# Attention value products issued in batches of up to eight key blocks, with twelve pairs of probability buffers, one buffer for the values and one for the copied row sums

## The reference, cut to what matters

```python
scores = jnp.einsum('brgtd,bgsd->brgts', qg, k) / jnp.sqrt(jnp.float32(HD))
bias = jnp.tril(diff)[None, None] * slopes[:, :, None, None]
causal = idx[None, :] <= idx[:, None]
scores = jnp.where(causal[None, None, None], scores + bias[None], -jnp.inf)
attn = jax.nn.softmax(scores, axis=-1)
out = jnp.einsum('brgts,bgsd->brgtd', attn, v)
...
gate = jnp.einsum('th,nh->tn', xt, Wg)
up = jnp.einsum('th,nh->tn', xt, Wu)
gelu = jnp.tanh(0.7978845608028654 * (gate + 0.044715 * gate ** 3)) * gate * 0.5 + gate * 0.5
inter = gelu * up
out = jnp.einsum('tn,hn->th', inter, Wd)
...
x = x + _L0_attn_ref(xn, ...) + _L0_ffn_ref(xn, ...)
```

## Time and profile before

| | |
|---|---|
| median of 3 runs | 1785.41 us (1784.62 to 1787.19) |
| the profiled execution's own time | 1784.39 us |
| its span, first to last instruction | 1782.6 us |
| TensorE busy | 1693.1 us (95%), 10368 matmuls |
| VectorE busy | 1340.1 us (75%) |
| ScalarE busy | 1075.6 us (60%) |
| GpSimd busy | 953.2 us (53%) |
| mean granted TensorE clock | 0.985 of full speed |

### The profile page before, as it was taken

How to read it: one execution, slowest core, us unless ns; L and a number is a source line. 1 busy time by engine, 2 the same in 40 slices (tenths; PEclk the granted TensorE clock), 3 DMA queues, 4 the chain that set the end, 5 groups by cost and what they waited for, 6 DMA issues and landing times. The chain is left out here.

```text
span 1782.6 us, 31010 instructions
## 1 busy us (share of the span) xinstructions
PE 1693.1 (95%) x10368; PEld 848.4 (48%) x10368; DVE 1340.1 (75%) x2785; ACT 1075.6 (60%) x1779; POOL 953.2 (53%) x801
## 2 busy tenths in 40 slices
PE   4989999999999999999999999999999999999947
PEld 3754444444444444444444444444444444444435
DVE  6867777777777777777777777777777777777728
ACT  2436757575757676675757575766757575757610
POOL 3315647374646556473746465564737464645617
PEclk9989999999999999999999999999999999999968
DMA  6770120302020201203021202012030203020154
GB/s 190 208 195 16 29 59 17 75 24 74 26 72 20 75 17 44 56 16 80 20 73 26 74 20 74 16 47 52 20 80 17 73 26 74 23 70 17 48 176 149
DMA packets 94971, 110.04 MB, mean 62 GB/s; under 512 B 39085, under 2 KB 58541, under 8 KB 93021
## 3 DMA queue, kind: packets, MB, share of 16 engines
q1 hardware_dynamic: 94812, 108.05, 22.3%
HBM read 72.74 MB, written 22.41 MB: 53 GB/s over the span
## 5 line engine op out<-in xcount | busy, mean ns | idle before, releaser
L1409 POOL TENSOR_TENSOR plo<-p,phi 128x512 f16<-128x512 f32 (+1 forms) x576 | 659.0, 1151 | 327.8 <-ACT phi L1241 324.9
L1234 ACT ACTIVATE p<-score_ps,pshift 128x512 f32<-128x512 f32 (+1 forms) x576 | 382.1, 663 | 308.0 <-DVE score_ps L1321 154.4
L1241 ACT ACTIVATE phi<-p 128x512 f16<-128x512 f32 (+1 forms) x576 | 349.9, 607 | 15.3
L1417 POOL TENSOR_TENSOR il<-prod,ih 128x512 f16<-128x512 f32 x128 | 160.8, 1256 | 352.5 <-DVE ih L1315 352.5
L1141 PE MATMUL score_ps<-qst,kst 128*128 128x512 f32 (+3 forms) x640 | 308.0, 498 | 12.1 <-ACT p L1234 10.7
L1336 DVE TENSOR_REDUCE mxp<-max_ps 128x1 f32<-128x512 f32 x256 | 175.3, 685 | 53.9 <-PE max_ps L1119 53.9
L1283 DVE TENSOR_TENSOR acc<-down_ps,acc 128x512 f32<-128x512 f32 x253 | 172.7, 683 | 52.2 <-PE down_ps L1087 50.3
L1107 PE MATMUL gate_ps<-xh,wh 128*128 128x512 f16 x512 | 199.1, 389 | 0.0
L1107 PE MATMUL up_ps<-xh,wh 128*128 128x512 f16 x512 | 198.4, 387 | 0.0
L1087 PE MATMUL down_ps<-wh,ih 128*128 128x512 f16 x506 | 196.1, 387 | 0.9 <-DVE acc L1283 0.9
L1107 PE MATMUL gate_ps<-xh,wl 128*128 128x512 f16 x512 | 194.8, 380 | 0.0
(11 more groups left out here) (197 smaller groups left out, 2910.2 us busy)
## 6 DMA issues: line engine op xcount, KB each, us to landing
qst<-q_parts SPq DMA_DIRECT2D x204, 64.0 KB
kst<-k_parts SPq DMA_DIRECT2D x48, 256.0 KB, 4.7
o<-oraw SPq DMA_DIRECT2D x192, 64.0 KB
vst<-v_parts SPq DMA_DIRECT2D x17, 512.0 KB, 6.1
q_parts<-o SPq DMA_DIRECT2D x24, 256.0 KB, 3.4
raw<-L_ffn_gate_W_packed_dram SPq DMA_DIRECT2D x18, 256.0 KB, 2.8
raw<-n_L_ffn_up_W_packed_dram SPq DMA_DIRECT2D x18, 256.0 KB, 3.1
raw<-L_ffn_down_W_packed_dram SPq DMA_DIRECT2D x18, 256.0 KB, 3.9
```

The source lines that it names most:

```text
L1234: nc.scalar.activation(p32[n % PR][:, 0:cols], score_ps[:, 0:cols], ACT.Exp, bias=pshift[:, 0:1]).then_inc(exp_done, 1)
L1241: nc.scalar.activation(phi[n % PP][:, 0:cols], p32[n % PR][:, 0:cols], ACT.Copy).then_inc(phi_done, 1)
L1409: nc.gpsimd.tensor_tensor(plo[n % PP][:, 0:cols], p32[n % PR][:, 0:cols], phi[n % PP][:, 0:cols], ALU.subtract).then_inc(plo_done, 1)
L1417: nc.gpsimd.tensor_tensor(il[w % 2][:, a, :], prod[a][:], ih[w % 2][:, a, :], ALU.subtract).then_inc(il_done, 1)
```

## The change

`BATCHES` now cuts a chunk's blocks into runs of up to eight: [0..2], [3..9], [10..17], [18..20], [21..28], [29..35], in slots 12, 20, 28, 32, 40 and 47. `phi` and `plo` have twelve buffers each. The products are the same in number and shape, 203 per head. What remains of the row sums behind the loop over the blocks starts in group 3 and goes round (3, 0, 1, 2, ...), and outside the first chunk the list of row-sum products is turned by half, so that the later blocks' sums are taken in the loop and the earlier ones' behind it. `vst` and `lraw` are single: the values of head i are loaded at the start of head i, once the value products of head i-1 are done, and the copy into `lraw` waits for the stores of the chunk before. In the preamble a tile `vst_too` takes the place that the second `vst` had.

```diff
@@ -93,4 +93,4 @@
 SLOT_OF = {n: s for s, n in SCORE_AT.items()}
-BATCHES = [list(range(n, min(n + 4, BLK_END[c]))) for c in range(NCH)
-           for n in range(BLK_END[c - 1] if c else 0, BLK_END[c], 4)]
+BATCHES = [list(range(n, min(n + 8, BLK_END[c]))) for c in range(NCH)
+           for n in range(BLK_END[c - 1] if c else 0, BLK_END[c], 8)]
 NBATCH = len(BATCHES)
@@ -200,3 +200,3 @@
             kst = [tile(f"kst{b}", [P, T], F32R) for b in range(2)]
-            vst = [tile(f"vst{b}", [P, NT, 4 * HD], F16) for b in range(2)]
+            vst = tile("vst", [P, NT, 4 * HD], F16)
 
@@ -204,3 +204,3 @@
             k_in = [sem(f"k_in{b}") for b in range(2)]
-            v_in = [sem(f"v_in{b}") for b in range(2)]
+            v_in = sem("v_in")
             q_in = [sem(f"q_in{c}") for c in range(NCH)]
@@ -391,3 +391,4 @@
         wq = [sb(f"wq{part}", [P, KT, C], F32R) for part in range(2)]
-        wkvs = [t[:].rearrange("p t n -> p (t n)").bitcast(F32R).rearrange("p (k n) -> p k n", k=KT) for t in vst]
+        vst_too = sb("vst_too", [P, NT, 4 * HD], F16)
+        wkvs = [t[:].rearrange("p t n -> p (t n)").bitcast(F32R).rearrange("p (k n) -> p k n", k=KT) for t in (vst, vst_too)]
 
@@ -917,3 +918,3 @@
         identr = sb("identr", [P, P], F32R)
-        PR, PP = 3, 8
+        PR, PP = 3, 12
         p32 = [sb(f"p32_{i}", [P, CH], F32) for i in range(PR)]
@@ -927,3 +928,3 @@
         oraw = [sb(f"oraw{i}", [P, CH], F32) for i in range(2)]
-        lraw = [sb(f"lraw{i}", [3 * HD, CH], F32) for i in range(2)]
+        lraw = sb("lraw", [3 * HD, CH], F32)
 
@@ -994,5 +995,5 @@
 
-                def load_v(i, b):
-                    sp.dma_start(vst[b][:], v_s[bass.ds(i // REP, 1)].rearrange("o p t d -> (o p) t d")
-                                 ).then_inc(v_in[b], 16)
+                def load_v(i):
+                    sp.dma_start(vst[:], v_s[bass.ds(i // REP, 1)].rearrange("o p t d -> (o p) t d")
+                                 ).then_inc(v_in, 16)
 
@@ -1009,3 +1010,2 @@
                     sp.wait_ge(stored, 32 * NCH)
-                load_v(0, 0)
                 for m in range(3):
@@ -1016,4 +1016,4 @@
                     sp.wait_ge(pv_done, after(i * NBATCH * PV_INCS))
+                    load_v(i)
                     load_k(nxt, 1 - par)
-                    load_v(nxt, 1 - par)
                     for c in range(NCH):
@@ -1047,3 +1047,3 @@
                     for q in range(1, LPARTS):
-                        sp.dma_start(l_s[par, q:q + 1, cols], lraw[c % 2][(q - 1) * HD:(q - 1) * HD + 1, :]
+                        sp.dma_start(l_s[par, q:q + 1, cols], lraw[(q - 1) * HD:(q - 1) * HD + 1, :]
                                      ).then_inc(o_out[c % 2], 16)
@@ -1065,3 +1065,2 @@
                 sp.wait_ge(k_in[0], K_FIRST + 48 * (HEADS // 2))
-                sp.wait_ge(v_in[0], 16 * (HEADS // 2 + 1))
                 for c in range(NCH):
@@ -1150,3 +1149,3 @@
                             mm = nc.tensor.matmul(
-                                bank[g * HD:(g + 1) * HD, tok:CH], vst[par][:, j, of * HD:(of + 1) * HD],
+                                bank[g * HD:(g + 1) * HD, tok:CH], vst[:, j, of * HD:(of + 1) * HD],
                                 src[n % PP][:, col:col + CH - tok], start=start, stop=n == BLK_END[c] - 1,
@@ -1161,4 +1160,6 @@
                         ones = [(n, src) for n in blocks for src in (phi, plo)]
+                        if c:
+                            ones = ones[count:] + ones[:count]
                         if batch == 0:
-                            pe.wait_ge(v_in[par], (pair + 1) * 16)
+                            pe.wait_ge(v_in, (i + 1) * 16)
                         if first:
@@ -1177,5 +1178,8 @@
                             mm.then_inc(pv_done, 1)
-                        for g, k in enumerate(range(count + 1, 2 * count)):
-                            product(l_ps, g, *ones[k], 1, first and c > 0).then_inc(pv_done, 1)
-                        product(o_ps, 3, *ones[count], 1, False).then_inc(pv_done, 1)
+                        for k in range(count):
+                            g = (k + 3) % 4
+                            mm = product(o_ps if g == 3 else l_ps, g, *ones[count + k], 1,
+                                         first and c > 0 and 0 < k < 4)
+                            if k + 4 >= count:
+                                mm.then_inc(pv_done, 1)
 
@@ -1253,3 +1257,5 @@
                         nc.scalar.activation(oraw[c % 2][:], o_ps[:], ACT.Copy, scale=oback[:, 0:1]).then_inc(oraw_done, 1)
-                        nc.scalar.activation(lraw[c % 2][:], l_ps[0:3 * HD, :], ACT.Copy).then_inc(oraw_done, 1)
+                        if i * NCH + c:
+                            act.wait_ge(o_out[(c + 1) % 2], ((i * NCH + c - 1) // 2 + 1) * 16 * O_DMAS)
+                        nc.scalar.activation(lraw[:], l_ps[0:3 * HD, :], ACT.Copy).then_inc(oraw_done, 1)
```

## The result

| | before | changed |
|---|---|---|
| median, us | 1786.3 (1784.62 to 1788.2, 4 runs) | 1768.44 (1767.93 to 1769.22, 4 runs) |
| profiled execution / its span, us | 1784.39 / 1782.6 | 1768.29 / 1766.5 |
| mean granted clock | 0.985 | 0.986 |
| steady head (mean of 15), us | 97.823 | 96.932 |

The ratio is 0.990 [0.9883, 0.9917]. "Steady head" is the distance from the first MLP product of a head to that of the next, as the mean of heads 2 to 16 (for the last, up to the first such product of the epilogue). The forecast was 1771.4 us and 0.87 to 0.88 less per head; measured is 0.892. The rows after are read at the same places as before.

What follows compares the result with a forecast made beforehand. The loop was taken as bound by the chain of TensorE's starts. Per head -0.84 - 0.32 + 0.29 = -0.87 to -0.88 us, times 16 is -14 us, giving 1771.4 us as the median, range 1766 to 1778.

Steps and rivals of the forecast that it cites:

- Term 1: Switches to narrow products and back: four fewer batches per head save 0.84 us, bounds 4 x 0.19 and 4 x 0.22.
- Term 2: Rounds within batches [3..9], [18..20], [29..35]: three half rounds fewer per head save 0.32 us, bounds 0 and 0.32.
- Term 3: Slot 17: without the batch of slot 16, TensorE waits for ScalarE's copy of the maxima, costing 0.29 us per head.
- The rival that it stays hidden: Slot 17's wait for the copy of the maxima stays covered, giving 1766.8 us; chance 0.13.
- Term 4: Slots losing a batch: other engines' idle time covers the 1.29 us shorter slots; cost 0, else 0.53 us per head.
- that rival: VectorE becomes the bound behind slots 24 and 36: 1779.9 us in full, some 1777 in part; chance 0.15.
- Term 5: Single `vst` and `lraw`: stores land 0.6 us before the tightest copy, values load in time; wait 0.
- its rival: The single `lraw` holds up ScalarE in slots 20 and 32, slower by up to 115 us; chance 0.03.
- Order of the groups: Rival: column groups served in program order, so group 3 holds back the others; 1.13 us more per head, 1789.5; chance 0.03.

Runs made afterwards that it cites:

- e1_fours: Changed kernel with batches of at most four blocks again, all else kept: 1780.5 us, ratio 0.9968 to the kernel before.
- e6_old_sums: Changed kernel without turning the list of row sums by half (part of its row sums is not the reference's): 1774.27 us, ratio 0.994.
- e2_split16: Changed kernel with batch [3..9] cut into [3..6] in slot 16 and [7..9] in slot 20: 1767.57 us, ratio 0.9895.
- e3_turn16: Changed kernel with the turn of the maxima issued before slot 16's first three MLP products instead of behind them: 1762.55 us, ratio 0.9869.
- e5_single: Kernel before with only the single buffers `vst` and `lraw`; batches of four, eight pairs, old row sums: 1783.24 us, ratio 0.9991.
- e7_tiles: Changed kernel issuing first tiles of a block for all four column groups, then the second tiles: 1769.02 us, ratio 0.9908.
- b0_before: The kernel before again, no edit, for a second profile: 1787.17 us, ratio 1.000.
- a0_after: The changed kernel again, no edit: 1768.1 us, ratio 0.990 to the kernel before.
- e4_turn8_16: Changed kernel with the turns in slots 8 and 16 ahead of the MLP products, and slot 8's copy ahead of ScalarE's square: 1762.66 us, ratio 0.9873.
- e8_values39: `e4_turn8_16` with batch [21..28] issued in slot 39 instead of slot 40: 1775.57 us, ratio 0.9942.
- e9_norm45: `e8_values39` with GpSimd's normalising product moved from slot 36 to slot 45: 1753.83 us, ratio 0.982.

## Why the prediction was right

**Term 1, boundaries, -0.84.** `e1_fours` measures 3 x 0.22 + 0.21 = 0.87, inside the bounds. The row of slot 24 had the price to 0.01; what it left out is 0.01 between the MLP products behind a batch, once per removed one. The full drain that the Trainium skill states ("TensorEngine Tiling (Array Packing)", Tiling Modes, Key Properties) would have been 1.3 by the prediction's estimate, twice 0.16 us per batch, and the runs deny that size.

**Term 2, half rounds, -0.32.** Measured 0.340 in the three slots, 0.02 beyond the bound that the prediction called the most there could be. `e6_old_sums` shows that they come from turning the list. Adding columns per group describes each batch to 0.01 us.

**Term 3, the wait, +0.29.** Measured 0.280. `e2_split16` shows that the batch had hidden it, `e3_turn16` that it is distance from turn to score. The rival that it stays hidden falls, by 4.5 us.

**Term 4, other engines, 0.** Nearly: the slack of VectorE was used to the last, as read, and costs TensorE nothing visible, so that rival falls. The 0.05 in slots 33 and 34 is ScalarE's, behind a batch that got shorter, a place that the prediction had not looked at since it priced only slots that lose a batch.

**Term 5, single buffers, 0.** `e5_single` confirms it for the loop, and its rival falls. The 1.9 us that the prediction took for the stores is the landing of a load, the nearest row; no row gives the landing of these stores. What is shown is that no copy waits for them.

**Order of the groups.** The prediction took the rule that matmuls start strictly in program order ("TensorE: Matmul & The Clock Gate", Part 3, of the Trainium skill) for the changed kernel alone, and its 1789.5 does not follow from it. Worked through the program in the same way, the rule gives the batch [7..9] of the kernel before 6.25 rounds, 1.35 us, where 0.98 was measured with the way out; and it gives 56 rounds per head before and 53.25 after, a gain and not a loss. So the total could not have told it apart. What does are the lengths of the batches, and `e7_tiles`: by the rule, issuing tile by tile saves 7.5 rounds, 1.6 us per head, and the head changed by 0.004.

**How close the head came.** The 0.892 against 0.87 to 0.88 is partly luck. Terms 1 to 3 were each off by 0.01 to 0.03, all in the direction of too little gain, and make 0.93 as measured; the 0.05 of slots 33 and 34, which the prediction did not have, takes most of that back.

**What is left.** 16 x 0.892 = 14.3 us, forecast 14; the median fell by 17.9 (to 1768.44 from 1786.3; the forecast had started from 1785.41). The forecast is 3 us too high, and the heads do not explain that. It lies outside the steady heads (profiled spans less the 15 heads: 315.2 us before, 312.5 after). By stretch, in us:

| | up to the first head | first head | after the last head |
|---|---|---|---|
| before | 120.4 | 101.9 | 92.9 |
| `b0_before` | 123.4 | 101.1 | 94.5 |
| changed | 122.7 | 99.6 | 90.2 |
| `a0_after` | 121.4 | 99.6 | 91.5 |
| `e5_single` | 120.3 | 100.1 | 92.8 |
| `e1_fours` | 120.3 | 101.1 | 93.7 |
| `e4_turn8_16` | 120.4 | 101.1 | 92.9 |

The first head and the epilogue are shorter in both profiles of the changed kernel than in both of before. But the kernel before alone varies by 3.7 in the sum, and `e4_turn8_16`, which has all of the change, looks like before in both stretches, so part of it is scatter. `e5_single` is 2.3 us below the median of before beside it with a ratio that just reaches 1.0; against the single buffers as the cause stands `e1_fours`, which has them too and comes to 315.0, as before. The cause stays open.

## What to carry to other kernels

Price a switch between wide and narrow products from one boundary in the timeline (here 0.2 us for there and back) and count boundaries; then look at each place that loses a batch for what it had covered. A result that goes through another engine and back (here 0.63 to the copy, 0.64 to the weights) wants that much of other work between, and moving it earlier pays only when what queues behind it, or ahead of it on the helper engine, has room: slot 16 gave all, slot 27 three quarters, slot 8 a third. A batch can be put where another wait would stand, which hides that wait, as soon as its own operands are ready; look at the engine that makes them (a wait of 1.48 us in `e8_values39`, 0.56 gained in `e9_norm45`).

## What the runs showed of the hardware

Products for different column groups run independently here: with the tiles of a block in another order the head changes by 0.004 of 96.9 us, and a batch lasts as long as the columns of its fullest group (0.216 us per 512, for 3.5, 4, 5, 8.5, 9 and 10 rounds, to 0.01 us). The switch costs 0.09 us each way beyond the ordinary distance, less than the 0.16 by which a product outlasts it.
